# The sum over the experts turned by VectorE's 32x32 transpose and a scratch in DRAM, in place of four TensorE transposes

## The chip, the cores and the metric

The kernel runs on one core of one Trainium2 chip. The metric is the device time of one execution in microseconds; lower is better. TensorE's clock has two levels here, 1.2 and 2.4 GHz; the profile gives the granted clock as a share of the higher one.

## The reference

The input is 16 sequences of 512 tokens with 128 features. Each sequence goes through two layers, each wrapped in layer norms:

```
x = x + layernorm(attn(layernorm(x)))     # attn: project to 64 states, a complex scan over time, project back, + D * u
x = x + layernorm(ffn(layernorm(x)))      # ffn: 8 experts, all of them computed for every token

g = x @ w_gate[e];  u = x @ w_up[e]       # 128 -> 512 for each expert e
out = sum over e of cw[e] * ((silu(g) * u) @ w_down[e])       # 512 -> 128
cw  = softmax(x @ w_router) * softmax(x @ w_gating / 0.1), normalised over the experts
```

The change concerns only the last step: the layer norm of `out`, its addition to the residual and the store.

## The kernel before, in words

A chunk is one sequence of 512 tokens; there are 16. Inside a chunk the experts run feature-major: features on the 128 partitions, 512 tokens along the free axis. A chunk has 32 **units** k = 0 to 31, four for each expert, each of 128 hidden features. In unit k TensorE makes `g` and `u` (three matmuls of 128x512 each, since every fp32 product is split into a high and a low part) and then the down projection `y` of unit k - 3 (three more). ScalarE makes `gate` = silu(g) and rounds `hid` to `hid_hi`; VectorE makes `hid` = gate * u, and `hid_lo` for half of the units; GpSimd makes `hid_lo` for the others (k mod 4 = 1 or 3). `g` and `u` each have two PSUM buffers, so u of unit k + 2 may not start before `hid` of unit k is done.

When the four units of an expert are through, VectorE's `weigh` multiplies `y` by the expert's token weights `cw_b` (into `acc` for expert 0, else into `y_part`) and GpSimd's `add_part` adds `y_part` to `acc`. The last addition of a chunk happens in unit 4 of the next chunk.

The rest runs between the units. What belongs to which unit is written out by hand in the tables `TENSOR_AT`, `SCALAR_AT`, `VECTOR_AT` and `GPSIMD_AT` (lines 44 to 52). In chunk c they hold, first, the attention layer and the routing of chunk c + 1 ("the mix"), and second, the end of chunk c - 1 ("the fin steps"), which are what the change touches:

- TensorE, unit 10, `turn_out`: four 128x128 transposes of `acc` to the PSUM tile `n_ps`, so that tokens lie on the partitions.
- VectorE, unit 10, `fin_stats` (four BN_STATS on `n_ps`) and `fin_mean_var` (five small operations); unit 11, `fin_shifts`, after GpSimd's `fin_rsqrt`.
- ScalarE, units 14 and 15, `fin_scale`: four activations from `n_ps` to `o_sb`.
- GpSimd, unit 14, `fin_residual`: adds `x1`.
- SyncE, after the fifth `spread_cw` of the chunk, `store_out`.

`n_ps` is one PSUM tile that the mix uses for its own turns as well. SyncE issues all transfers in the order of its code: in a chunk the load of the next input, the store of the weights `cw_t` to a scratch, and eight `spread_cw`, each of which broadcasts one row of weights over all partitions, and waits until its buffer (one of four) is free.

Ahead of the first chunk there is a start (about 45 us) in which VectorE builds the table `trig` and runs the mix of chunk 0. TensorE has little to do there and is kept busy with matmuls whose results nobody reads: `keep_warm(n)` with the counts in `WARM`, and one call of `keep_warm_mixed`.

Of the kernel before, what the change touches and what calls it, by code (L numbers as in the profile page):

```python
# [47 lines left out]
VECTOR_AT = {"weights": 1, "stats_x": 1, "var_x": 2, "norm_x": 3, "lo_x": 7, "enter": 8, "scan": 9,  # L48
             "fin_stats": 10, "fin_var": 10, "fin_shift": 11, "leave": 12, "lo_w": 13, "y": 15, "stats_y": 16, "var_y": 16,
             "shift": 18, "stats_x1": 22, "var_x1": 22, "norm_x1": 24, "lo_xe": 26, "softmax": 27, "exps": 30,  # L50
             "products": 31}
GPSIMD_AT = {"rstd_x": 2, "fin_rstd": 11, "fin_add": 14, "rstd_y": 16, "residual": 18, "rstd_x1": 22}
LN_EPS = 1e-5
# [4 lines left out]
SMALL = 32  # L58
PROJ = P + D + 2 * E

POOL_LO = (1, 3)
# [15 lines left out]
def build(nc, x_in, proj_in, a_in, sines_in, d_in, wgate_in, wup_in, wdown_in, out):  # L77
# [5 lines left out]
    wdown_v = wdown_in.rearrange("e (b p) h -> e p b h", p=P)  # L83

    cw_dram = nc.dram_tensor("cw_scratch", [2, E * NT, P], f32, kind="Internal").ap()

    with ExitStack() as ctx:
# [28 lines left out]
        z_sb = sb("z_sb", [P, NT, D])  # L116
        x1 = sb("x1", [P, 2, NT, D])
        o_sb = sb("o_sb", [P, NT, D])
        trig = sb("trig", [P, SEQ])

# [25 lines left out]
        w_hi_done, w_lo_done = sem("w_hi_done"), sem("w_lo_done")  # L146
        const_ready, flat_ready = sem("const_ready"), sem("flat_ready")
        proj_split, omega_ready, trig_link, trig_ready = sem("proj_split"), sem("omega_ready"), sem("trig_link"), sem("trig_ready")
# [31 lines left out]
        def _(sp):  # L180
# [16 lines left out]
            def spread_cw(c, par, e, first):  # L197
# [39 lines left out]
        def _(pe):  # L237
# [28 lines left out]

            def keep_warm_mixed():


                y, w, x = y_ps[1], proj_hi[:, 0:P], act_hi[:]  # L270
                flat = hid_hi[:, 0, :]
                for i in range(4):
                    nc.tensor.matmul(y[0:32, :], w[:, 0:32], x, start=True, stop=True)
                for i in range(4):
                    nc.tensor.matmul(y[:], proj_hi[0:NS, 0:P], act_hi[0:NS, :], start=True, stop=True)
                for i in range(4):
                    nc.tensor.matmul(y[:], w, act_hi[:, 0:1].broadcast_to([P, SEQ]), start=True, stop=True)
                for off in (0, 4, 8):
                    for i in range(4):
                        nc.tensor.matmul(y[:, 0:SEQ - 8], w, act_hi[:, off:off + SEQ - 8], start=True, stop=True)  # L280
                pe.wait_ge(flat_ready, 2)
                for i in range(4):
                    nc.tensor.matmul(y[:], flat[:, 0:P], flat, start=True, stop=True)
                keep_warm(3)

# [19 lines left out]
            def mix_turn_y(c, first):  # L305
                pe.wait_ge(y_ready, c + 1)
                if not first:
                    pe.wait_ge(fin_z, c - 1)
                turn(n_ps, lambda j: y_sb[:, j * P:(j + 1) * P]).then_inc(y_turned, 1)
# [17 lines left out]

            def turn_out(c, par, tail=False, last=False):
                pe.wait_ge(part_added, ADDS * (c + 1))
                if last:  # L330
                    pe.wait_ge(fin_z, c)
                elif tail:
                    pe.wait_ge(cw_t_ready, c + 2)
                else:
                    pe.wait_ge(act_lo_ready, 2 * c + 5)
                turn(n_ps, lambda j: acc[:, par, j * P:(j + 1) * P]).then_inc(fin_turned, 1)
# [48 lines left out]
            def body(c, par, first, last):  # L385
                for k in range(UNITS):
# [9 lines left out]
                    if not last:  # L396
# [18 lines left out]
            turn_out(NCHUNK - 1, (NCHUNK - 1) % 2, last=True)  # L415


        @block.scalar
        def _(act):
# [131 lines left out]
        def _(dve):  # L551
# [86 lines left out]
            def mix_stats_x1(c, par):  # L638
                dve.wait_ge(x1_ready, c + 1)
                measure(lambda j: x1[:, par, j, :], stats, mix_link)  # L640

            def mix_norm_x1(c, par):
                dve.wait_ge(rstd_ready, 3 * c + 3)
                normalise(xn, lambda j: x1[:, par, j, :]).then_inc(xn_ready, 1)

# [45 lines left out]
            def mix_weights(c):  # L691
# [9 lines left out]
                                        wide(den[:], E), ALU.mult).then_inc(cw_ready, 1)  # L701

            def fin_stats(c):
                dve.wait_ge(fin_turned, c + 1)
                measure(lambda j: n_ps[:, j * P:(j + 1) * P], stats2, fin_link)
# [161 lines left out]
            def body(c, par, first, last):  # L867
                for k in range(UNITS):
# [16 lines left out]
                    if not last:  # L885
# [36 lines left out]
                        if k == VECTOR_AT["products"]:  # L922
                            mix_products(c + 1)
                    if not first:
                        if k == VECTOR_AT["fin_stats"]:
                            fin_stats(c - 1)
                        if k == VECTOR_AT["fin_var"]:
                            fin_mean_var(c - 1)
                        if k == VECTOR_AT["fin_shift"]:
                            fin_shifts(c - 1)  # L930
# [10 lines left out]
                                    ALU.add).then_inc(part_added, 1)  # L941
            fin_stats(NCHUNK - 1)
            fin_mean_var(NCHUNK - 1)
            fin_shifts(NCHUNK - 1)
            for j in range(NT):
                if j < NT - 1:
                    dve.wait_ge(fin_tile, j + 1)
                else:
                    dve.wait_ge(fin_z, NCHUNK)
                last = nc.vector.tensor_tensor(o_sb[:, j, :], x1[:, end, j, :], o_sb[:, j, :], ALU.add)  # L950
            last.then_inc(fin_ready, 1)
# [3 lines left out]
        def _(pool):  # L955
# [10 lines left out]
            def mix_residual(c, par):  # L966
                pool.wait_ge(z_ready, c + 1)
                nc.gpsimd.tensor_tensor(x1[:, par], x_sb[:], z_sb[:], ALU.add).then_inc(x1_ready, 1)

# [4 lines left out]
            def fin_residual(c, par):  # L974
                pool.wait_ge(fin_z, c + 1)
                nc.gpsimd.tensor_tensor(o_sb[:], x1[:, par], o_sb[:], ALU.add).then_inc(fin_ready, 1)

# [101 lines left out]
```

## Time and profile before

| | before |
|---|---|
| three runs, us | 1173.66, 1175.09, 1175.84 |
| median, us | 1175.09 |
| the profiled execution's own time, us | 1174.75 |
| span of its trace, us | 1172.9 |
| mean granted clock of TensorE | 0.992 |
| TensorE matmul busy, share of the span | 97% |
| VectorE busy | 79% |
| ScalarE busy | 58% |
| GpSimd busy | 54% |
| DMA queue of SyncE, share of 16 engines | 13.4% |

The profiled execution took 0.34 us less than the median, and 1.85 us of its time lie outside its span. Matmuls overlap in the records (a 128x512 matmul is shown with some 390 ns, while the next one starts 227 ns after it), so the cost of a matmul is read from the distance of starts or from the chain that ended last, not from its own duration.

### The profile page before, as it was taken

To read this page: it belongs to the slowest core of one execution; us is meant where nothing else is said; L and a number is where in the kernel's file an instruction comes from. 1 tells how busy PE (TensorE), PEld (TensorE's weight loads), DVE (VectorE), ACT (ScalarE), POOL (GpSimd) and SP (SyncE) were. 2 spreads that over 40 slices of the span, in tenths; PEclk is the share of its full clock that TensorE was granted. 3 is DMA by queue.
4 is the path that set the end of the run, shared out by engine and by line. 5 is a ranking of instruction groups with operands and counts; after the bars stand their busy time and mean duration, and the time that the engine had idled before them with its cause. 6 is when DMAs were issued, how large, how long until landed. Compare 5 with 4: busy or idle time off the path is not lost.

```text
span 1172.9 us, 16867 instructions
## 1 busy us (share of the span) xinstructions
PE 1143.5 (97%) x5190; PEld 943.3 (80%) x5190; DVE 928.8 (79%) x2032; ACT 677.4 (58%) x1293; POOL 636.2 (54%) x496
## 2 busy tenths in 40 slices
PE   5899999999999999999999999999999999999996
PEld 4678888888888888888888888888888888888885
DVE  8788787787878878787887878778787887878665
ACT  3366565656556566565656656565655656556553
POOL 4467464555546455564655546455554645556453
PEclk8999999999999999999999999999999999999999
DMA  4230110101111020110101111010111102011110
GB/s 122 64 111 25 46 45 34 40 20 46 46 43 49 1 72 19 45 46 37 41 15 57 35 46 46 32 42 19 46 46 41 50 1 72 19 46 37 37 46 10
DMA packets 43097, 49.75 MB, mean 42 GB/s; under 512 B 3424, under 2 KB 24576, under 8 KB 43008
## 3 DMA queue, kind: packets, MB, share of 16 engines
q1 hardware_dynamic: 43008, 48.67, 13.4%
q8 instruction: 43, 0.70, 0.2%
q14 instruction: 46, 0.38, 0.1%
HBM read 44.20 MB, written 4.46 MB: 41 GB/s over the span
## 4 chain that ended last, share of the span: by engine, by line
PE 95%; DVE 3%; issue 1%; POOL 0%; ACT 0%; DMA 0%; POOLq 0%; SPq 0%; ACTq 0%; DVEq 0%
PE g L240 10%; PE u L240 10%; PE u L242 10%; PE u L241 10%; PE g L242 10%; PE g L241 10%; PE y L242 10%; PE y L240 10%; PE y L241 10%; PE n_ps L247 2%; PE m_ps L240 1%; PE m_ps L242 1%; PE m_ps L241 1%; PE y L263 1%; PE m_ps L321 1%
## 5 line engine op out<-in xcount | busy, mean ns | idle before, releaser
L982 POOL TENSOR_TENSOR hid_lo<-hid,hid_hi 128x512 fp32r<-128x512 f32 x255 | 342.2, 1342 | 394.5 <-ACT hid_hi L483 394.3
L477 ACT ACTIVATE gate<-g 128x512 f32<-128x512 f32 x512 | 306.3, 598 | 363.0 <-PE g L242 360.5
L723 DVE TENSOR_TENSOR hid<-gate,u 128x512 f32<-128x512 f32 x512 | 349.2, 682 | 176.9 <-ACT gate L477 121.6
L483 ACT ACTIVATE hid_hi<-hid 128x512 fp32r<-128x512 f32 x512 | 320.6, 626 | 29.4 <-DVE hid L723 28.7
L240 PE MATMUL g<-xe_hi,w_hi 128*128 128x512 f32 x512 | 207.8, 406 | 0.0
L729 DVE TENSOR_TENSOR hid_lo<-hid,hid_hi 128x512 fp32r<-128x512 f32 x257 | 205.7, 800 | 0.4
L240 PE MATMUL u<-xe_hi,w_hi 128*128 128x512 f32 x512 | 200.0, 391 | 2.3 <-DVE hid L723 2.3
L240 PE MATMUL y<-hid_hi,w_hi 128*128 128x512 f32 x512 | 199.8, 390 | 0.2 <-ACT hid_hi L483 0.2
L242 PE MATMUL y<-hid_hi,w_lo 128*128 128x512 f32 x512 | 199.8, 390 | 0.0
L242 PE MATMUL g<-xe_hi,w_lo 128*128 128x512 f32 x512 | 199.6, 390 | 0.0
L241 PE MATMUL g<-xe_lo,w_hi 128*128 128x512 f32 x512 | 199.6, 390 | 0.0
L242 PE MATMUL u<-xe_hi,w_lo 128*128 128x512 f32 x512 | 199.5, 390 | 0.0
L241 PE MATMUL y<-hid_lo,w_hi 128*128 128x512 f32 x512 | 199.3, 389 | 0.0
L241 PE MATMUL u<-xe_lo,w_hi 128*128 128x512 f32 x512 | 199.2, 389 | 0.0
L989 POOL TENSOR_TENSOR acc<-acc,y_part 128x512 f32<-128x512 f32 x111 | 159.2, 1434 | 3.1 <-DVE y_part L738 3.1
L240 PEld LDWEIGHTS u<-xe_hi,w_hi 128*128 128x128 f32 x512 | 96.1, 188 | 23.5 <-DVE hid L723 3.1
L240 PEld LDWEIGHTS y<-hid_hi,w_hi 128*128 128x128 f32 x512 | 96.1, 188 | 20.8 <-ACT hid_hi L483 0.6
L242 PEld LDWEIGHTS g<-xe_hi,w_lo 128*128 128x128 f32 x512 | 96.2, 188 | 20.6
L242 PEld LDWEIGHTS u<-xe_hi,w_lo 128*128 128x128 f32 x512 | 96.1, 188 | 20.5
L242 PEld LDWEIGHTS y<-hid_hi,w_lo 128*128 128x128 f32 x512 | 96.1, 188 | 20.5
L241 PEld LDWEIGHTS u<-xe_lo,w_hi 128*128 128x128 f32 x512 | 96.1, 188 | 20.3
L241 PEld LDWEIGHTS y<-hid_lo,w_hi 128*128 128x128 f32 x512 | 96.1, 188 | 20.1
(155 smaller groups left out, 1146.6 us busy)
## 6 DMA issues: line engine op xcount, KB each, us to landing
cw_b<-cw_scratch SPq DMA_DIRECT2D x128, 256.0 KB, 3.6
x_sb<-x_in SPq DMA_DIRECT2D x16, 256.0 KB, 4.0
x_out<-o_sb SPq DMA_DIRECT2D x16, 256.0 KB, 2.3
stage<-wgate_in SPq DMA_DIRECT2D x8, 256.0 KB, 2.7
stage<-wup_in SPq DMA_DIRECT2D x8, 256.0 KB, 3.0
stage<-wdown_in SPq DMA_DIRECT2D x8, 256.0 KB, 3.6
cw_scratch<-cw_t SPq DMA_DIRECT2D x16, 16.0 KB, 1.4
proj<-proj_in SPq DMA_DIRECT2D x1, 136.0 KB, 2.5
```

What stands on the lines that cost most here:

```text
L240: nc.tensor.matmul(dst, w_h, x_h, start=start, stop=False)
L241: nc.tensor.matmul(dst, w_h, x_l, start=False, stop=False)
L242: return nc.tensor.matmul(dst, w_l, x_h, start=False, stop=stop)
L247: last = nc.tensor.transpose(dst[:, j * P:(j + 1) * P], src(j), ident[:])
L263: last = nc.tensor.matmul(y_ps[1][:, 0:2 * P].rearrange("p (a b) -> p a b", a=2), ident[:], ident[:].unsqueeze(1).broadcast_to([P, 2, P]), ...
L321: last = nc.tensor.matmul(m_ps[:, at:at + 2 * E], xe_lo[:, par, t], router[:, 0, :], start=False, stop=True)
L477: nc.scalar.activation(gate[:, k % 2, :], g_ps[k % 2][:], ACT.Silu).then_inc(gate_ready, 1)
L483: nc.scalar.activation(hid_hi[:, k % RING, :], hid[:, k % RING, :], ACT.Copy).then_inc(hi_ready, 1)
L723: nc.vector.tensor_tensor(hid[:, k % RING, :], gate[:, k % 2, :], u_ps[k % 2][:], ALU.mult).then_inc(hid_ready, 1)
L729: nc.vector.tensor_tensor(hid_lo[:, k % RING, :], hid[:, k % RING, :], hid_hi[:, k % RING, :].bitcast(f32), ALU.subtract).then_inc(lo_dve, 1)
L982: nc.gpsimd.tensor_tensor(hid_lo[:, k % RING, :], hid[:, k % RING, :], hid_hi[:, k % RING, :].bitcast(f32), ALU.subtract).then_inc(lo_pool, 1)
L989: nc.gpsimd.tensor_tensor(acc[:, par, :], acc[:, par, :], y_part[:, e % 2, :], ALU.add).then_inc(part_added, 1)
```

## The change

For chunks 0 to 14 the four TensorE transposes are replaced. In unit 6 of the next chunk VectorE transposes `acc` in 32x32 blocks into `acc_t` (`fin_turn`). Each block is now turned in itself but stands in the wrong place. SyncE then stores `acc_t` with four transfers (`turn_blocks`), each from 32 partitions, in pieces of 32 fp32 values (128 bytes), to a scratch in DRAM in token-major order, and loads the scratch back as `ffn`, tokens on partitions (`load_blocks`). The fin steps read `ffn` in SBUF instead of `n_ps`, and are moved: `fin_stats` and `fin_mean_var` from unit 10 to 14, `fin_shifts` from 11 to 15, `fin_rsqrt` from 11 to 15, `fin_scale` from 14 and 15 to 19 and 20, `fin_residual` from 14 to 21, and `store_out` to the end of the chunk's eight `spread_cw`. `x1` gets three buffers instead of two. The last chunk keeps its TensorE transposes. In the start, `keep_warm_mixed` is replaced by `keep_warm(18)`, and 24 matmuls (`keep_warm_split`) are put where TensorE was idle before the first projection; the two VectorE instructions that filled an operand of `keep_warm_mixed` are gone.

```diff
-TENSOR_AT = {"turn_cw": 4, "turn_x": 5, "bu": 9, "turn_out": 10, "c": 15, "turn_y": 16, "turn_xe": 26,
+TENSOR_AT = {"turn_cw": 4, "turn_x": 5, "bu": 9, "c": 15, "turn_y": 16, "turn_xe": 26,
-SCALAR_AT = {"cw_t": 3, "hi_x": 8, "du": 8, "hi_w": 13, "fin_a": 14, "fin_b": 15, "z_a": 18, "z_b": 18,
+SCALAR_AT = {"cw_t": 3, "hi_x": 8, "du": 8, "hi_w": 13, "fin_a": 19, "fin_b": 20, "z_a": 18, "z_b": 18,
...
+FIN_STORED = 16 * (D // SMALL)
+X1S = 3
...
+    out_dram = nc.dram_tensor("out_scratch", [SEQ, D], f32, kind="Internal").ap()
...
+            def turn_blocks(c):
+                sp.wait_ge(fin_turned, c + 1)
+                if c > 0:
+                    sp.wait_ge(fin_loaded, 16 * c)
+                blocks = out_dram.rearrange("(b c) (a r) -> a c b r", c=SMALL, r=SMALL)
+                for a in range(D // SMALL):
+                    sp.dma_start(blocks[a], acc_t[a * SMALL:(a + 1) * SMALL, :].rearrange("c (b r) -> c b r", r=SMALL)
+                                 ).then_inc(fin_stored, 16)
+
+            def load_blocks(c):
+                sp.wait_ge(fin_stored, FIN_STORED * (c + 1))
+                if c > 0:
+                    sp.wait_ge(fin_z, c)
+                sp.dma_start(ffn[:], out_dram.rearrange("(j p) d -> p j d", p=P)).then_inc(fin_loaded, 16)
...
                 for e in range(E):
                     spread_cw(c, par, e, first)
-                    if e == 4 and not first:
+                    if e == 3 and not first:
+                        turn_blocks(c - 1)
+                        load_blocks(c - 1)
+                    if e == E - 1 and not first:
                         store_out(c - 1)
...
-            def keep_warm_mixed():
...
+            def keep_warm_split():
+                w = proj_hi[:, 0:P]
+                for i in range(8):
+                    nc.tensor.matmul(y_ps[1][:, 0:SEQ - P], w, act_hi[:, 0:SEQ - P], start=True, stop=True)
+                for i in range(8):
+                    nc.tensor.matmul(y_ps[1][:].rearrange("p (a t) -> p a t", a=2), w,
+                                     act_hi[:, 0:HALF].unsqueeze(1).broadcast_to([P, 2, HALF]), start=True, stop=True)
+                for i in range(8):
+                    nc.tensor.matmul(y_ps[1][:].rearrange("p (t a) -> p t a", a=2), w,
+                                     act_hi[:, 0:HALF].unsqueeze(2).broadcast_to([P, HALF, 2]), start=True, stop=True)
...
             keep_warm(WARM[1])
+            pe.wait_ge(act_hi_ready, 1)
+            keep_warm_split()
             pe.wait_ge(proj_split, 2)
...
-            keep_warm_mixed()
+            keep_warm(WARM[3])
...
-                    if k == TENSOR_AT["turn_out"] and not first:
-                        turn_out(c - 1, 1 - par, tail=last)
...
-                    last = nc.scalar.activation(o_sb[:, j, :], n_ps[:, j * P:(j + 1) * P], ACT.Identity,
+                    last = nc.scalar.activation(o_sb[:, j, :], ffn[:, j, :], ACT.Identity,
...
+            def fin_turn(c, par):
+                dve.wait_ge(part_added, ADDS * (c + 1))
+                if c > 0:
+                    dve.wait_ge(fin_stored, FIN_STORED * c)
+                nc.vector.transpose(acc_t[:], acc[:, par, :]).then_inc(fin_turned, 1)
+
             def fin_stats(c):
+                dve.wait_ge(fin_loaded, 16 * (c + 1))
+                measure(lambda j: ffn[:, j, :], stats2, fin_link)
```

TensorE, around unit 10 of a chunk that has a chunk before it (y of unit 7, then what follows up to g of unit 11). Before:

```order
L240 MATMUL y<-hid_hi,w_hi 128x512
L241 MATMUL y<-hid_lo,w_hi 128x512
L242 MATMUL y<-hid_hi,w_lo 128x512
L247 MATMUL n_ps<-ident,acc 128x128 x4
L240 MATMUL g<-xe_hi,w_hi 128x512
L241 MATMUL g<-xe_lo,w_hi 128x512
L242 MATMUL g<-xe_hi,w_lo 128x512
```

and now:

```order
L263 MATMUL y<-hid_hi,w_hi 128x512
L264 MATMUL y<-hid_lo,w_hi 128x512
L265 MATMUL y<-hid_hi,w_lo 128x512
L263 MATMUL g<-xe_hi,w_hi 128x512
L264 MATMUL g<-xe_lo,w_hi 128x512
L265 MATMUL g<-xe_hi,w_lo 128x512
```

The four transposes are gone; the matmuls on both sides are the same. VectorE, from the last step of the scan in unit 12 (`v_sb`) over the `hid` of unit 13 to that of unit 16, before:

```order
L619 TENSOR_TENSOR v_sb<-sum_sb,trig 128x512
L723 TENSOR_TENSOR hid<-gate,u 128x512
L729 TENSOR_TENSOR hid_lo<-hid,hid_hi 128x512
L624 TENSOR_TENSOR act_lo<-v_sb,act_hi 128x512
L723 TENSOR_TENSOR hid<-gate,u 128x512 x2
L729 TENSOR_TENSOR hid_lo<-hid,hid_hi 128x512
L628 TENSOR_TENSOR y_sb<-m_ps,y_sb 128x512
L723 TENSOR_TENSOR hid<-gate,u 128x512
```

and now, from the `hid` of unit 14:

```order
L743 TENSOR_TENSOR hid<-gate,u 128x512
L566 BN_STATS stats<-ffn 128x6 x4
L573 TENSOR_TENSOR mv<-stats 128x8
L574 TENSOR_TENSOR var_eps<-stats 128x4
L578 TENSOR_TENSOR mv<-mv,pair_mean 128x8
L579 SCALAR_TENSOR_TENSOR var_eps<-var_eps 128x4
L584 SCALAR_TENSOR_TENSOR var_eps<-mv,var_eps 128x4
L743 TENSOR_TENSOR hid<-gate,u 128x512
L749 TENSOR_TENSOR hid_lo<-hid,hid_hi 128x512
L638 TENSOR_TENSOR y_sb<-m_ps,y_sb 128x512
L600 SCALAR_TENSOR_TENSOR shift<-mv,rstd 128x4
L743 TENSOR_TENSOR hid<-gate,u 128x512
```

The four BN_STATS and the five small operations of the fin steps now stand between the `hid` of units 14 and 15, and `fin_shifts` (the one on `shift`) behind `y_sb`; before they stood in units 10 and 11. SyncE, one whole chunk, before:

```order
L182 DMA x_sb<-x_in 128x4x128
L195 DMA cw_scratch<-cw_t 32x128
L204 DMA cw_b<-cw_scratch 128x512 x5
L208 DMA x_out<-o_sb 128x4x128
L204 DMA cw_b<-cw_scratch 128x512 x3
```

and now:

```order
L187 DMA x_sb<-x_in 128x4x128
L200 DMA cw_scratch<-cw_t 32x128
L209 DMA cw_b<-cw_scratch 128x512 x4
L217 DMA out_scratch<-acc_t 32x16x32 x4
L224 DMA ffn<-out_scratch 128x4x128
L209 DMA cw_b<-cw_scratch 128x512 x4
L228 DMA x_out<-o_sb 128x4x128
```

The four stores and the load stand between the fourth and the fifth broadcast, and the store of the output moved behind the eighth.

## Rows read from the trace of the kernel before

**Rows 1.** The page: span, and busy us (share of the span) by engine

```profile
span 1172.9 us, 16867 instructions
PE 1143.5 (97%) x5190; PEld 943.3 (80%) x5190; DVE 928.8 (79%) x2032; ACT 677.4 (58%) x1293; POOL 636.2 (54%) x496
```

**Rows 2.** Busy time in a window: start:end, length, then busy us by engine

```profile
120.00:1100.00 980.00, 980.00 (x4488) 812.05 (x4487) 789.09 (x1719) 582.84 (x1112) 533.82 (x408) 1.00 0.12 38
```

**Rows 3.** The chain that ended last, in order of time: start us, us, what

```profile
212.65 0.44 PE n_ps L247 x4
226.02 0.44 PE n_ps L247 x4
...
295.69 0.44 PE n_ps L247 x4
```

**Rows 4.** Timeline, units 4 to 7 of a chunk: start us, us, instruction [idle before]

```profile
201.84 1.81 POOL L989 TENSOR_TENSOR acc<-acc,y_part 128x512 f32<-128x512 f32 x1
...
203.19 0.69 DVE L723 TENSOR_TENSOR hid<-gate,u 128x512 f32<-128x512 f32 x1 [0.70 <-ACT gate L477]
205.24 0.69 DVE L723 TENSOR_TENSOR hid<-gate,u 128x512 f32<-128x512 f32 x1 [1.36 <-PE u L242]
```

**Rows 5.** Groups by line: VectorE operations of 128x512 from SBUF to SBUF

```profile
L615 DVE TENSOR_TENSOR_SCAN sum_sb<-v_sb 128x512 f32<-128x512 f32 x16 | 20.6, 1288 | 0.0
...
L624 DVE TENSOR_TENSOR act_lo<-v_sb,act_hi 128x512 fp32r<-128x512 f32 x15 | 11.3, 752 | 0.0
...
L759 DVE CAST hid_hi<-hid 128x512 fp32r<-128x512 f32 x1 | 0.4, 428 | 0.0
```

**Rows 6.** DMA: queue, issues, and the last store's window (last columns: clock, DMA share, GB/s)

```profile
q1 hardware_dynamic: 43008, 48.67, 13.4%
...
x_sb<-x_in SPq DMA_DIRECT2D x16, 256.0 KB, 4.0
x_out<-o_sb SPq DMA_DIRECT2D x16, 256.0 KB, 2.3
...
1170.30:1172.90 2.60, 0.50 0.34 101
```

**Rows 7.** Timeline of VectorE, fin_stats at unit 10, then units 14 to 16

```profile
214.15 0.89 DVE L556 BATCH_NORM_STATS2 stats<-n_ps 128x6 f32<-128x128 f32 x4
...
215.73 0.69 DVE L723 TENSOR_TENSOR hid<-gate,u 128x512 f32<-128x512 f32 x1
...
222.71 0.69 DVE L723 TENSOR_TENSOR hid<-gate,u 128x512 f32<-128x512 f32 x1 [0.80 <-ACT gate L477]
...
224.02 0.69 DVE L628 TENSOR_TENSOR y_sb<-m_ps,y_sb 128x512 f32<-128x512 f32 x1
225.43 0.69 DVE L723 TENSOR_TENSOR hid<-gate,u 128x512 f32<-128x512 f32 x1 [0.72 <-PE u L242]
```

**Rows 8.** Timeline, ScalarE and VectorE and TensorE, unit 15 and units 18 to 21

```profile
222.99 0.80 ACT L468 ACTIVATE o_sb<-n_ps,shift,rstd 128x128 f32<-128x128 f32 x2
...
231.81 1.50 ACT L441 ACTIVATE z_sb<-n_ps,shift,rstd 128x128 f32<-128x128 f32 x4 [1.42 <-DVE shift L590]
...
234.20 0.62 ACT L477 ACTIVATE gate<-g 128x512 f32<-128x512 f32 x1
...
233.84 0.69 DVE L723 TENSOR_TENSOR hid<-gate,u 128x512 f32<-128x512 f32 x1 [2.06 <-ACT gate L477]
...
233.16 0.39 PE L240 MATMUL u<-xe_hi,w_hi 128*128 128x512 f32 x1
...
235.20 0.39 PE L240 MATMUL u<-xe_hi,w_hi 128*128 128x512 f32 x1
```

**Rows 9.** The start: windows of 1 us, and VectorE's last step before mix_c

```profile
17.00:18.00 1.00, 0.00 (x0) 0.00 (x0) 1.00 (x2) 0.00 (x0) 1.00 (x2) 0.89 0.00 0
...
42.00:43.00 1.00, 1.00 (x4) 0.86 (x5) 0.38 (x2) 0.06 (x1) 0.00 (x0) 0.50 0.31 16
...
27.57 0.42 DVE L838 TENSOR_TENSOR act_lo<-v_sb,act_hi 128x256 fp32r<-128x256 f32 x1
```

More of the change, by code:

```diff
@@ L41 @@
 PIECES = WCOLS // F
-TENSOR_AT = {"turn_cw": 4, "turn_x": 5, "bu": 9, "turn_out": 10, "c": 15, "turn_y": 16, "turn_xe": 26,
+TENSOR_AT = {"turn_cw": 4, "turn_x": 5, "bu": 9, "c": 15, "turn_y": 16, "turn_xe": 26,
              "logits": 27}
-SCALAR_AT = {"cw_t": 3, "hi_x": 8, "du": 8, "hi_w": 13, "fin_a": 14, "fin_b": 15, "z_a": 18, "z_b": 18,
+SCALAR_AT = {"cw_t": 3, "hi_x": 8, "du": 8, "hi_w": 13, "fin_a": 19, "fin_b": 20, "z_a": 18, "z_b": 18,
              "hi_xe": 26, "silus": 28}
 VECTOR_AT = {"weights": 1, "stats_x": 1, "var_x": 2, "norm_x": 3, "lo_x": 7, "enter": 8, "scan": 9,
-             "fin_stats": 10, "fin_var": 10, "fin_shift": 11, "leave": 12, "lo_w": 13, "y": 15, "stats_y": 16, "var_y": 16,
+             "fin_turn": 6, "fin_stats": 14, "fin_var": 14, "fin_shift": 15, "leave": 12, "lo_w": 13, "y": 15, "stats_y": 16, "var_y": 16,
              "shift": 18, "stats_x1": 22, "var_x1": 22, "norm_x1": 24, "lo_xe": 26, "softmax": 27, "exps": 30,
              "products": 31}
-GPSIMD_AT = {"rstd_x": 2, "fin_rstd": 11, "fin_add": 14, "rstd_y": 16, "residual": 18, "rstd_x1": 22}
+GPSIMD_AT = {"rstd_x": 2, "fin_rstd": 15, "fin_add": 21, "rstd_y": 16, "residual": 18, "rstd_x1": 22}
 LN_EPS = 1e-5
@@ L116, in build @@
         z_sb = sb("z_sb", [P, NT, D])
-        x1 = sb("x1", [P, 2, NT, D])
+        x1 = sb("x1", [P, X1S, NT, D])
         o_sb = sb("o_sb", [P, NT, D])
+        acc_t, ffn = sb("acc_t", [P, SEQ]), sb("ffn", [P, NT, D])
         trig = sb("trig", [P, SEQ])
@@ L265, in keep_warm @@
                 return last
-            def keep_warm_mixed():
[L270 to L284, printed above, removed]
+            def keep_warm_split():
[8 more added lines that the diff above has]
+                                     act_hi[:, 0:HALF].unsqueeze(2).broadcast_to([P, HALF, 2]), start=True, stop=True)
             def mix_turn_x(c):
@@ L306, in mix_turn_y @@
                 pe.wait_ge(y_ready, c + 1)
-                if not first:
-                    pe.wait_ge(fin_z, c - 1)
                 turn(n_ps, lambda j: y_sb[:, j * P:(j + 1) * P]).then_inc(y_turned, 1)
@@ L326, in mix_turn_cw, with turn_out_last @@
                 nc.tensor.transpose(n_ps[:, 0:P], cw_pad[:], ident[:]).then_inc(cw_turned, 1)
-            def turn_out(c, par, tail=False, last=False):
+            def turn_out_last(c, par):
                 pe.wait_ge(part_added, ADDS * (c + 1))
[L330 to L335, printed above, removed]
+                pe.wait_ge(cw_t_ready, c + 1)
                 turn(n_ps, lambda j: acc[:, par, j * P:(j + 1) * P]).then_inc(fin_turned, 1)
@@ L414, in _ @@
                 down(NCHUNK - 1, k, False, last_unit=k == UNITS - 1)
-            turn_out(NCHUNK - 1, (NCHUNK - 1) % 2, last=True)
+            turn_out_last(NCHUNK - 1, (NCHUNK - 1) % 2)
         @block.scalar
@@ L639, in mix_stats_x1 @@
                 dve.wait_ge(x1_ready, c + 1)
[L640 removed]
+                measure(lambda j: x1[:, c % X1S, j, :], stats, mix_link)
             def mix_norm_x1(c, par):
                 dve.wait_ge(rstd_ready, 3 * c + 3)
[L644 removed]
+                normalise(xn, lambda j: x1[:, c % X1S, j, :]).then_inc(xn_ready, 1)
             def mix_lo_xe(c, par):
@@ L924, in body @@
                     if not first:
+                        if k == VECTOR_AT["fin_turn"]:
+                            fin_turn(c - 1, 1 - par)
                         if k == VECTOR_AT["fin_stats"]:
@@ L941, in _ @@
                                     ALU.add).then_inc(part_added, 1)
-            fin_stats(NCHUNK - 1)
+            fin_stats_last(NCHUNK - 1)
             fin_mean_var(NCHUNK - 1)
@@ L949, in _ @@
                     dve.wait_ge(fin_z, NCHUNK)
-                last = nc.vector.tensor_tensor(o_sb[:, j, :], x1[:, end, j, :], o_sb[:, j, :], ALU.add)
+                last = nc.vector.tensor_tensor(o_sb[:, j, :], x1[:, (NCHUNK - 1) % X1S, j, :], o_sb[:, j, :], ALU.add)
             last.then_inc(fin_ready, 1)
@@ L967, in mix_residual @@
                 pool.wait_ge(z_ready, c + 1)
-                nc.gpsimd.tensor_tensor(x1[:, par], x_sb[:], z_sb[:], ALU.add).then_inc(x1_ready, 1)
+                nc.gpsimd.tensor_tensor(x1[:, c % X1S], x_sb[:], z_sb[:], ALU.add).then_inc(x1_ready, 1)
             def fin_rsqrt(c):
@@ L975, in fin_residual @@
                 pool.wait_ge(fin_z, c + 1)
-                nc.gpsimd.tensor_tensor(o_sb[:], x1[:, par], o_sb[:], ALU.add).then_inc(fin_ready, 1)
+                nc.gpsimd.tensor_tensor(o_sb[:], x1[:, c % X1S], o_sb[:], ALU.add).then_inc(fin_ready, 1)
             def hid_low(c, k, first):
```

7 lines of the change are left out of this document (3 added, 4 removed).

## The prediction

> **What bounds the kernel now.** I read the page first. TensorE's matmuls fill 97% of a span of 1172.9 us, VectorE 79% of it [rows 1]. Next the busy time of the long middle stretch: from 120 to 1100 us TensorE is busy for 980.00 of 980.00 us at full granted clock [rows 2], so outside the start and the tail there is no idle time of TensorE to win, and a chunk gets shorter only if TensorE is given less to do. The chain that ended last agrees: it goes from matmul to matmul, and the turn of `y_sb` in it comes back after 295.69 - 226.02 = 69.67 us, the length of a chunk [rows 3]. The other engines matter only where they are late enough to stop TensorE, so the timelines of VectorE and ScalarE around each moved step are read for one thing, how much time is left before the matmul that needs them.
>
> **What is removed.** Four transposes of `acc` take 0.44 us of the chain [rows 3]. They go from 15 of 16 chunks, since the last keeps its own: 15 x 0.44 = 6.6 us. They are shown in the chain with nothing beside them, and TensorE has no gap before the next g, so all of it comes off if nothing else becomes late.
>
> **The block transpose on VectorE (unit 6).** No such operation is in the trace. The nearest, 128x512 from SBUF to SBUF, run from 0.43 us (the cast, the fastest) through 0.75 us (a tensor_tensor) to 1.29 us (the scan) [rows 5]. I take 0.7. It stands between the `hid` of units 6 and 7, where VectorE is idle for 1.36 us waiting for TensorE's u; the last addition to `acc`, for which it has to wait, ends at 201.84 + 1.81 = 203.65, and the `hid` before it is over at about 203.8 [rows 4]. So it starts at once, and even 1.29 us fits into the gap. It costs the path nothing. Without the gap it would cost nothing either until the `hid` behind it is about two units late. What ends is at about 204.5 on the clock of that chunk.
>
> **The transfers.** Four stores, 32 partitions x 16 pieces = 512 pieces of 128 bytes each, 2048 in all, then a load of 512 pieces of 512 bytes like that of `x_sb`. The path needs `ffn` in unit 14, behind a `hid` after which VectorE is free at 222.71 - 0.80 = 221.9 now [rows 7], and 0.44 earlier once the transposes are gone, or a little before that: about 221.2. The final store of the output has 512 pieces of 512 bytes too; it lands in 2.3 us, with 0.34 x 2.60 = 0.88 us of work for each of the 16 engines: 27 ns for each of its 32 pieces [rows 6]. The mean over all packets of the kernel is 0.134 x 1172.9 / (43008 / 16) = 58 ns [rows 6], for packets of 1.1 KB. The stores are 128 pieces per engine, so 3.5 us at 27 ns and 7.4 us at 58 ns; I take 7.4, as the pieces are small. With the fixed part of a store, 2.3 - 0.9 = 1.4 us, and 4.0 us for the load [rows 6], `ffn` is there at 204.5 + 1.4 + 7.4 + 4.0 = 217.3, or 213.4 at the low price, 4 to 8 us before it is wanted. SyncE stands still for all of this, and what is queued behind it are the fifth broadcast of weights, whose row is first used in unit 24, some 20 us on, and the later ones; nobody waits for these. Behind the eighth, `store_out` waits for GpSimd's addition in unit 21; behind that stands the load of the next input, used one unit into the next chunk, again about ten units off.
>
> The Trainium skill, "DMA: Bandwidth & Descriptors", section Specifications, says that transfers under 512 bytes fall below line rate because the engine reads, modifies and writes; "VectorE: DVE Perf Modes", section The three transpose paths, warns that a plain copy that transposes by strides is 19 times slower than the crossbar's. No row here shows either. Taken on the 27 ns piece as an estimate, 19 times would be 0.5 us a piece and 66 us of stores in a chunk, which would make the change a disaster; but the pieces here are 32 contiguous values, the elements having been turned by VectorE before, so I do not take it.
>
> **The moved fin steps.** In unit 10, statistics and variance take 214.15 to 215.73, 1.58 us, on a VectorE that is then late for the next `hid` [rows 7]. That goes. In unit 14 they come between two `hid` with 0.80 us of idle time, ahead of `y_sb`, before which and after which VectorE waits again, 0.72 us [rows 7]. TensorE needs `y_sb` for its turn at 226.02, now 0.44 earlier at 225.6, and it is ready at 224.02 + 0.69 = 224.7 [rows 3, 7]. Started at 221.2, `fin_mean_var` is over at 222.8, and the `hid` of unit 15, which could start at 222.71 - 0.44 = 222.3, starts half a microsecond late; the idle time ahead of `y_sb` and behind it takes this up. Nothing on the path. On ScalarE the four activations, 0.80 us a pair, move from units 14 and 15 to 19 and 20, right behind the mix's own four of 1.50 us, after which ScalarE is catching up [rows 8]. The `hid` of unit 19 ends at 234.53 and TensorE wants it at 235.20: 0.7 us to spare, the tightest place. The first pair comes after the silu of that unit, so it delays the next: silu of unit 20 from 234.20 to 235.0, its `hid` to about 236.3; u of unit 22 starts at 235.20 + (235.20 - 233.16) = 237.24 [rows 8]: 0.9 us to spare. `hid_lo` of unit 19 on GpSimd keeps about as much. Cost 0; without this cover it would be up to 0.8 us per pair.
>
> **The start.** TensorE is idle in the window at 17 us, and its clock falls to half there [rows 9]. The 24 new matmuls fill about 24 x 0.227 = 5 us ahead of that, at the distance of matmuls in a unit, (235.20 - 233.16) / 9 = 0.227 us [rows 8]. The chain there runs through VectorE, though: its last step before the second projection ends at 27.57 + 0.42 = 27.99 [rows 9], whatever TensorE's clock. If the clock stays up, 0.2 us are won in the projection; if it falls later instead, its three matmuls cost 3 x 0.227 = 0.7 us more at the lower level. In the window at 42 us, just ahead of the first unit, the clock is at half again [rows 9]; six passes of keep_warm and a first g at that level are worth some 1.5 us either way. I take 0, with -1.5 to +1.5.
>
> **The sum.** 1174.75 (the profiled execution: span 1172.9 and 1.85 around it) - 6.6 = 1168.15. The median is 0.34 above that execution, so against the median 1168.5. I give 1168.4.
>
> **The rivals.** *Slow small pieces (slower).* If `ffn` is late, VectorE, which works in order, stands at `fin_stats` with `hid` of unit 15, `hid_lo` and `y_sb` queued behind it, 1.58 + 3 x 0.6 = 3.4 us of work that must end by 225.6. So `ffn` may come up to 222.2. This leaves 222.2 - 4.0 - 1.4 - 204.5 = 12.3 us for 128 pieces: 96 ns each is where it turns. A write that first reads costs two mean packets, 116 ns: 20 ns too much, 2.6 us a chunk, 15 chunks, +38 - 6.6, so 1207. For it: no row has small writes at all. Against: even a mean packet is well below. The read-modify-write of the skill would be this case. Chance 0.10.
>
> *The wait moves to units 19 to 22 (about no gain).* For it: 0.7 to 0.9 us to spare, and operations of VectorE that are held up while GpSimd works; GpSimd's addition has moved there too. If it stops TensorE by 0.3 to 0.5 us a chunk, 4.5 to 7.5 us come back: 1173 to 1176. Against: nowhere in the middle stretch is TensorE stopped now, with the same 0.7 us. Chance 0.12; a third of this with most of the gain kept.
>
> *The start gives it back:* priced above, within 1.5 us; it is inside the likeliest case's range, not a case of its own.
>
> **How the numbers follow.** The plain case, everything hidden, has the remaining 0.78. Its own range is 1168.4 with -1.5 and +1.5 for the start and about 0.5 for the runs: 1166.4 to 1170.4. To leave out no more than 2 in 10 the range reaches up into the second case, to 1171.8. A measurement of this kernel tells 0.2%, 2.35 us, from no change. Faster by more than that (below 1172.7): all of the plain case and a third of the second, 0.82. Within it: half of the second, 0.06. Slower: the first rival and the rest, 0.12.
>
> **What would show it.** In the profile after: chunks of 69.67 - 0.44 = 69.2 us; the middle stretch again without idle time of TensorE; the transpose on VectorE at 0.4 to 1.3 us with an idle gap left behind it; the stores landed within 9 us and `fin_stats` not waiting for the load; the second projection in the start at 28 us. Wrong would be: a wait of `fin_stats` for the transfer of `ffn` of more than about 1 us, or waits of TensorE for `hid` or `hid_lo` in units 19 to 22, or the first g later than 45 us by more than 1.5.

## The result, and the profile after

| | before | after |
|---|---|---|
| median of 9 runs each, taken together, us | 1174.46 | 1170.8 |
| lowest and highest | 1173.18, 1176.11 | 1169.59, 1171.37 |
| ratio | | 0.9967 [0.9957, 0.9977] |
| the profiled execution, its own time and its span | 1174.75, 1172.9 | 1171.27, 1169.4 |

The changed kernel is faster by 3.66 us, where 6.6 were forecast. The interval of the ratio allows 2.7 to 5.1 us. The time is inside the range given, 2.4 us above the forecast, but 0.4 us above the range of the prediction's plain case, which ended at 1170.4. Its page, with the columns of [rows 1, 6]:

```profile
span 1169.4 us, 16900 instructions
PE 1144.2 (98%) x5156; PEld 940.8 (80%) x5156; DVE 946.0 (81%) x2045; ACT 673.4 (58%) x1293; POOL 640.3 (55%) x496
...
q1 hardware_dynamic: 82608, 56.54, 16.4%
...
x_out<-o_sb SPq DMA_DIRECT2D x16, 256.0 KB, 2.2
out_scratch<-acc_t SPq DMA_DIRECT2D x60, 64.0 KB, 2.3
ffn<-out_scratch SPq DMA_DIRECT2D x15, 256.0 KB, 2.7
```

And the middle stretch, as in [rows 2]:

```profile
120.00:1100.00 980.00, 980.00 (x4451) 807.82 (x4450) 809.49 (x1738) 580.75 (x1115) 538.97 (x409) 1.00 0.16 46
```

TensorE has fewer instructions, VectorE is busy for 17 us more, the packets have almost doubled, and still TensorE is the engine that is never without work in the middle. Busy time, though, does not show whether each matmul took as long as before; the chain does. First the turn of `y_sb` of chunk 0 in the kernel before, then in the changed kernel, and there one chunk from turn to turn (the turn of `y_sb`, the one for `xe`, that of the next input, and `y_sb` again):

```profile
85.89 0.44 PE n_ps L247 x4
...
87.19 0.44 PE n_ps L270 x4
...
226.50 0.44 PE n_ps L270 x4
247.40 0.51 PE n_ps L270 x4
271.53 0.44 PE n_ps L270 x4
295.88 0.44 PE n_ps L270 x4
```

This shows two things against the forecast. A chunk lasts 295.88 - 226.50 = 69.38 us, not 69.2: of [rows 3]'s 69.67 only 0.29 is gone. And the turn of chunk 0 stands at 87.19, where the chain of before has it at 85.89: the start lost 1.30 us. From there to the end 4.8 us were won. 4.8 - 1.3 = 3.5 is the difference of the two spans.

The steps on which the prediction spent most words, on the timeline of VectorE and SyncE of the changed kernel:

```profile
204.75 0.70 DVE L717 STREAM_TRANSPOSE acc_t<-acc 128x512 f32<-128x512 f32 x1
205.48 2.74 SPq L217 DMA_DIRECT2D out_scratch<-acc_t  x4
206.19 0.69 DVE L743 TENSOR_TENSOR hid<-gate,u 128x512 f32<-128x512 f32 x1 [0.73 <-ACT gate L487]
...
210.47 0.38 SPq L224 DMA_DIRECT2D ffn<-out_scratch  x1
...
222.19 0.86 DVE L566 BATCH_NORM_STATS2 stats<-ffn 128x6 f32<-128x128 f32 x4
```

The block transpose takes 0.70 us and leaves 0.73 us of its gap idle. The load is issued 210.47 - 204.75 = 5.7 us after the transpose began, and lands 2.7 us later, at 213.2; `fin_stats` comes 9 us after that and waits for nothing. The transfers are not where the missing 2.9 us are.

### The profile page after: what moved, and what is told of

The parts are those of the page before. It is cut to its first block, busy times and chain, and to the rows that moved or that the text cites. A ratio compares the mean times of both kernels' runs of the same rounds, so it can differ in the third digit from the quotient of the medians.

```text
span 1169.4 us, 16900 instructions
## 1 busy us (share of the span) xinstructions
PE 1144.2 (98%) x5156; PEld 940.8 (80%) x5156; DVE 946.0 (81%) x2045; ACT 673.4 (58%) x1293; POOL 640.3 (55%) x496
## 4 chain that ended last, share of the span: by engine, by line
PE 95%; DVE 3%; issue 1%; POOL 0%; ACT 0%; DMA 0%; POOLq 0%; SPq 0%; ACTq 0%; DVEq 0%
PE g L263 10%; PE u L263 10%; PE u L265 10%; PE u L264 10%; PE g L264 10%; PE g L265 10%; PE y L263 10%; PE y L265 10%; PE y L264 10%; PE n_ps L270 2%; PE m_ps L263 1%; PE m_ps L265 1%; PE m_ps L264 1%; PE m_ps L335 1%; PE y L286 1%; PE m_ps L336 1%
## 5 line engine op out<-in xcount | busy, mean ns | idle before, releaser
L749 DVE TENSOR_TENSOR hid_lo<-hid,hid_hi 128x512 fp32r<-128x512 f32 x257 | 202.3, 787 | 1.8
```

The lines of the kernel that those rows point to most:

```text
L749: nc.vector.tensor_tensor(hid_lo[:, k % RING, :], hid[:, k % RING, :], hid_hi[:, k % RING, :].bitcast(f32), ALU.subtract).then_inc(lo_dve, 1)
```

## The experiments

All were timed beside the kernel before on their own chip; its medians there were 1174.86 (the first four kernels below the changed one), 1176.01 (the next four) and 1174.88 (the last four). "Turn 0" is the turn of `y_sb` of chunk 0 in the chain, which reads the start; "chunk" is the mean distance of that turn over the middle chunks; "rest" is what the profiled execution's span has left behind turn 0, which leaves the start out.

| kernel | median (lowest to highest, n), us | ratio to before | turn 0 | chunk | rest |
|---|---|---|---|---|---|
| before | 1174.46 (1173.18 to 1176.11, 9) | 1 | 85.89 | 69.67 | 1087.01 |
| after | 1170.8 (1169.59 to 1171.37, 9) | 0.9967 [0.9957, 0.9977] | 87.19 | 69.37 | 1082.21 |
| after, old start | 1168.37 (1167.83 to 1169.89, 5) | 0.9952 [0.9939, 0.9964] | 84.42 | 69.35 | 1082.08 |
| before, new start | 1175.65 (1175.07 to 1176.2, 11) | 1.001 [1.0001, 1.0019] | 86.68 | | 1087.12 |
| scale and addition later | 1168.08 (1167.9 to 1168.99, 5) | 0.9948 [0.9935, 0.996] | 85.99 | 69.21 | 1080.11 |
| addition later | 1168.51 (1167.92 to 1168.96, 5) | 0.9949 [0.9936, 0.9961] | 87.09 | 69.20 | 1080.01 |
| addition later, old start | 1167.8 (1166.14 to 1168.09, 5) | 0.9933 [0.9921, 0.9946] | 85.91 | 69.21 | 1080.09 |
| stores four times | 1170.32 (1169.69 to 1171.14, 4) | 0.9957 [0.9942, 0.9973] | 86.25 | 69.38 | 1082.45 |
| stores eight times | 1287.82 (1285.74 to 1289.51, 4) | 1.0956 [1.0939, 1.0973] | 86.17 | | |
| filler up to the turn | 1169.16 (1168.98 to 1169.38, 5) | 0.9947 [0.9935, 0.996] | 84.90 | 69.37 | 1082.30 |
| without the split matmuls | 1170.09 (1169.47 to 1171.06, 5) | 0.9957 [0.9944, 0.9969] | 87.05 | 69.35 | 1082.15 |
| addition later, filler to the turn | 1167.13 (1166.98 to 1168.43, 5) | 0.9932 [0.9919, 0.9946] | 84.91 | 69.23 | 1080.59 |
| the same without the split matmuls | 1166.62 (1166.43 to 1166.78, 5) | 0.9926 [0.9913, 0.9938] | 84.82 | 69.21 | 1079.98 |
| before, new start, filler to the turn | 1173.87 (1173.13 to 1174.43, 11) | 0.9991 [0.9983, 1.0] | 84.95 | | 1087.15 |

### The start, alone and taken out

The changed kernel with the old start, and the old kernel with the new one:

```diff
-            keep_warm_split()
...
-            keep_warm(WARM[3])
+            keep_warm_mixed()
...
+            nc.vector.memset(hid[:, 0, :], 0.5).then_inc(flat_ready, 1)
+            nc.vector.tensor_copy(hid_hi[:, 0, :], hid[:, 0, :]).then_inc(flat_ready, 1)
```

> The changed kernel with the start of before put back: keep_warm_mixed and its two VectorE instructions instead of the 24 new matmuls and keep_warm(18); the chunks are those of the changed kernel. In the profiles so far the start ends 1.30 us later in the changed kernel, because TensorE's clock comes back to full at 48.0 us instead of 46.0, while the chunks give 4.8 us. Theory A, the new start is the cause: the first turn of y_sb is back at about 85.9 us and the median about 1.3 us below the changed kernel, 1169.5. Theory B, the moment at which the clock comes back scatters from execution to execution whatever the start: median within 0.6 us of the changed kernel, 1170.8, and spans that scatter by up to 2 us in both.

> The kernel before with only the new start; the chunks and the four TensorE transposes are those of before. Theory A: about 1.3 us above the kernel before, 1175.8. Theory B: within 0.6 us of it, 1174.5.

The new start costs about 1.2 us on the old kernel (1.001, with an interval from 0.1 to 2.2 us), and taking it out of the changed one gives 1.8 us by the ratios (0.9967 to 0.9952, whose intervals overlap). In both chains the turn at about 30 us stands level (30.02 before, 30.06 after); the windows behind it show where the time goes, first of the changed kernel:

```profile
30.00:41.00 11.00, 8.72 (x41) 7.29 (x41) 7.25 (x26) 2.28 (x6) 6.95 (x7) 1.00 0.25 73
38.00:40.00 2.00, 0.49 (x3) 0.09 (x1) 0.84 (x3) 0.00 (x0) 1.67 (x2) 1.00 0.31 94
...
42.00:48.00 6.00, 6.00 (x17) 4.73 (x17) 1.07 (x3) 1.19 (x2) 0.00 (x0) 0.50 0.57 175
```

then of the one with the old start:

```profile
30.00:41.00 11.00, 11.00 (x36) 7.66 (x34) 7.82 (x25) 1.74 (x5) 6.96 (x7) 0.69 0.24 73
...
42.00:48.00 6.00, 5.84 (x30) 4.76 (x31) 2.66 (x7) 2.27 (x5) 0.00 (x0) 1.00 0.58 175
```

and of the kernel before, which has the old start too:

```profile
42.00:48.00 6.00, 6.00 (x26) 5.02 (x27) 2.16 (x6) 1.20 (x2) 0.00 (x0) 0.74 0.57 175
```

`keep_warm(18)` is over at 38.5 us, TensorE is nearly idle until the turn for `xe` at 41.9, and then the first matmuls of the experts run with a granted clock of 0.50, the lower level of 1.2 GHz, until 48: 17 of them in a stretch that holds 30 at 2.4 GHz. In the run with the old start the filler ran at a mixed clock, took longer, and reached up to 41.3; the window from 42 to 48 us has 1.00. But the old start is not safe either: the profiled execution of before had 0.74 there, and so did that of the kernel with the addition later and the old start, both with turn 0 at 85.9. So the old start can come out as in the second profile or as in the third. That the start differs from one execution to the next was the rival, and both hold. Over the profiles the clock of 42 to 48 us and turn 0 go together: 0.50 and 0.51 with 87.19 and 87.05, 0.72 to 0.74 with 85.89 to 86.68, 1.00 with 84.42.

### The split matmuls left out

```diff
-            pe.wait_ge(act_hi_ready, 1)
-            keep_warm_split()
```

> The changed kernel without the 24 new matmuls of the start (keep_warm_split); keep_warm(18) stays. Theory: what counts in the start is how long TensorE is busy ahead of the first unit, from 30 to 41 us, so these 24 matmuls between 13 and 18 us are worth little: median within 0.7 us of the changed kernel, 1170.8. Rival: with TensorE idle from 13 to 22 us the clock comes back late and slow filler reaches 41 us by itself, as in one run of the old start: 1169.3 or less.

The same time, and turn 0 at 87.05 for 87.19. The matmuls fill the gap ahead of the first projection, but the chain there runs through VectorE, as the prediction said.

### Filler up to the turn

```diff
-WARM = (13, 3, 6, 18, 3)
+WARM = (13, 3, 6, 24, 3)
```

> The changed kernel with keep_warm(24) instead of keep_warm(18) behind the first turn of y_sb, so that TensorE is busy until about 41.2 us instead of 38.5, and idles hardly at all before the first unit. Theory: the granted clock then stays full from 40 to 48 us, three passes of keep_warm and the first g and u run at the upper level, and the first turn of y_sb in unit 16 comes at 84.4 to 85.0 us (87.2 in the changed kernel, 84.4 in the run with the old start, where a low clock from 30 to 34 us had stretched the same kind of filler to 41.3). Time 1168.3 to 1169.0. Rival: the clock falls anyway (it is another idle stretch that counts), or the longer filler holds up the turn: 1170.8 or more.

```profile
30.00:41.00 11.00, 10.95 (x53) 9.57 (x53) 7.26 (x25) 2.28 (x6) 6.96 (x7) 1.00 0.25 73
...
42.00:48.00 6.00, 5.84 (x30) 4.62 (x31) 2.72 (x8) 1.74 (x4) 0.00 (x0) 1.00 0.60 175
```

Six more matmuls nobody reads, no gap, a clock of 1.00 and turn 0 at 84.90. In the runs the ratio goes from 0.9967 to 0.9947. In all four kernels with this filler the clock of 42 to 48 us is 1.00 and turn 0 stands between 84.82 and 84.95. The median is slightly above the 1169.0 that was expected at most. So the gap ahead of the turn was the cause of the loss in the start: with it the clock of 42 to 48 us lay between 0.50 and 0.74 in nine profiles, without it at 1.00 in five. It makes some of the scatter too: these five runs lie within 0.4 us and those of the best version below within 0.35, where the nine of the changed kernel spread over 1.8; but two others with the filler still spread over 1.3 and 1.45.

### The fin steps, both later, and the addition alone

For the 0.29 instead of 0.44 us a chunk the suspects were the steps moved into units 19 to 21: ScalarE's two pairs, or GpSimd's addition.

```diff
-SCALAR_AT = {..., "fin_a": 19, "fin_b": 20, ...}
+SCALAR_AT = {..., "fin_a": 23, "fin_b": 24, ...}
-GPSIMD_AT = {..., "fin_add": 21, ...}
+GPSIMD_AT = {..., "fin_add": 26, ...}
```

> The changed kernel with fin_scale in units 23 and 24 instead of 19 and 20, and fin_residual in unit 26 instead of 21. Theory: of the 0.44 us that the removed transposes give in each chunk, 0.15 come back in units 26 and 27, because the fin steps in units 19 to 21 make VectorE's normalisation of x1 in unit 24 late (245.0 us instead of 243.0 on the clock of the chunk), so that the turn for xe and the logits wait. If so, the chunk takes 69.22 us instead of 69.37, and the time is 15 x 0.15 = 2.2 us below the changed kernel, 1168.6. Rival: the lateness comes from fin_stats in unit 14, or from the missing 0.44 us itself; then the chunk stays at 69.37 and the time at 1170.8.

And with the second of the two lines alone:

> As the run before, but only GpSimd's fin_residual is moved (unit 26 instead of 21); fin_scale stays on ScalarE in units 19 and 20. If GpSimd's addition is the cause (it delays hid_lo of unit 21 and the reciprocal root of x1's variance), nearly all of the 0.15 us a chunk comes back: 1168.8. If ScalarE's two pairs are the cause (they delay the silu and so hid of units 20 to 22), it stays near 69.37 us a chunk, 1170.8. I expect half: the normalisation starts some 1 us earlier, and the chunk takes about 69.28.

I had given each half of the loss, and that missed: the addition alone brings the chunk to 69.20, and moving ScalarE's pairs as well adds nothing that can be measured. The same four turns of the chain with the addition in unit 26:

```profile
226.33 0.44 PE n_ps L270 x4
247.23 0.44 PE n_ps L270 x4
271.23 0.44 PE n_ps L270 x4
295.53 0.44 PE n_ps L270 x4
```

From the turn of `y_sb` to that for `xe` both kernels take 20.90 us. From there to the turn of the next input it is 24.00 here and 24.13 in the changed kernel, of which 0.07 is the longer turn itself (0.51 for 0.44); the next piece is 24.30 here and 24.35 there. What makes the difference stands on the timelines of GpSimd and VectorE; of the changed kernel, units 21 to 25:

```profile
239.12 1.75 POOL L995 TENSOR_TENSOR o_sb<-x,o_sb 128x512 f32<-128x512 f32 x1
240.82 1.29 POOL L1001 TENSOR_TENSOR hid_lo<-hid,hid_hi 128x512 fp32r<-128x512 f32 x1
...
242.76 1.02 POOL L983 TENSOR_TENSOR rstd<-var_eps,half 128x4 f32<-128x4 f32 x1 [0.65 <-DVE var_eps L584]
...
241.12 1.01 DVE L573 TENSOR_TENSOR mv<-stats 128x8 f32<-128x8 f32 x1
...
245.03 2.17 DVE L595 TENSOR_SCALAR xn<-x,mv,rstd 128x128 f32<-128x128 f32 x4
```

and of the one with the addition in unit 26:

```profile
239.24 1.48 POOL L1001 TENSOR_TENSOR hid_lo<-hid,hid_hi 128x512 fp32r<-128x512 f32 x1 [0.22 <-ACT hid_hi L493]
241.78 1.02 POOL L983 TENSOR_TENSOR rstd<-var_eps,half 128x4 f32<-128x4 f32 x1 [1.05 <-DVE var_eps L584]
...
248.81 1.29 POOL L995 TENSOR_TENSOR o_sb<-x,o_sb 128x512 f32<-128x512 f32 x1
...
240.99 0.17 DVE L573 TENSOR_TENSOR mv<-stats 128x8 f32<-128x8 f32 x1
...
244.06 2.17 DVE L595 TENSOR_SCALAR xn<-x,mv,rstd 128x128 f32<-128x128 f32 x4
```

In unit 21 the addition stands ahead of GpSimd's `hid_lo` and pushes it from 239.24 to 240.82 (the two chunks stand 0.17 us apart). VectorE's small step of the variance of `x1` now falls beside that `hid_lo` and takes 1.01 us for 0.17, in each of the chunks 1 to 14 (with the addition in unit 26 it is 0.17 in all of them). It ends at 242.13, when that `hid_lo` does (242.11). On the clock of the chunk the root on GpSimd behind it is 0.8 us later, and the normalisation `xn` too; it ends at 245.03 + 2.17 = 247.20, just as TensorE comes to the turn at 247.40. With the addition in unit 26 it ends at 246.23, for a turn at 247.23: a microsecond early. The list of waits counts what TensorE's weight loads lost, in the changed kernel:

```profile
PEld n_ps L270 <- DVE xn L595: 7.1, 16, 1.9
...
PEld m_ps L335 <- issue: 3.4, 15, 0.2
```

and with the addition in unit 26:

```profile
PEld n_ps L270 <- DVE xn L595: 3.0, 2, 1.9
...
PEld m_ps L335 <- issue: 0.2, 1, 0.2
```

The first entry is the transposes waiting for `xn`, the second the logits' loads of 0.2 us each. The two waits that are left stand in chunk 0, which has no fin steps; the other 14 are the chunks 1 to 14, which have both the fin steps and the mix.

Both remedies were put together, first with the old start, then with the longer filler, and the filler also on the kernel before, whose transposes stay on TensorE.

> The two causes together: GpSimd's fin_residual in unit 26, and the start of before. If they are independent, the time is that of the run with only the addition moved, 1168.5, less the 1.1 to 1.8 us that the old start was worth: 1166.7 to 1167.4. Against the kernel before this is the whole 15 x 0.44 = 6.6 us and a little more.

> The changed kernel with both mends: GpSimd's fin_residual in unit 26, and keep_warm(24). Theory, the two are independent: 1169.16 - 2.2 = 1166.9, with the first turn of y_sb at 84.9 us and chunks of 69.21 us.

> The kernel before, its four TensorE transposes in every chunk, with the new start and keep_warm(24). It is the fair rival of the run before in this list: the same start, only the turn differs. Theory: the first turn of y_sb at 84.4 to 84.9 us instead of 85.9, so 1173.5; and the difference to the run with both mends is 15 x 0.45 = 6.7 us, all of what the removed transposes take.

The first came out slightly above what was expected. The last two differ only in the replaced transposes and where the fin steps stand, with a start of the same length in both (84.91 and 84.95): 1173.87 - 1167.13 = 6.74 us, that is 0.45 for each of 15 chunks, with about 1.9 us either way by the intervals of the two ratios. This is the term of the prediction, measured by itself. By the rest behind turn 0 it is 1087.15 - 1080.59 = 6.6; but that profiled execution has 0.4 us more behind its last chunk than the other four with the addition in unit 26, whose rest is 1080.0 to 1080.1; against those it is 7.0 to 7.2.

### Repeated stores

The prediction's rival of slow small pieces turned at 96 ns a piece. The stores were issued four and eight times, each time to a scratch of its own, and the load waits for all:

```diff
-                for a in range(D // SMALL):
-                    sp.dma_start(blocks[a], ...
+                for n, a in [(n, a) for n in range(REPEAT) for a in range(D // SMALL)]:
+                    sp.dma_start(blocks[n, a], ...
```

> The changed kernel with the four stores of the turned blocks issued four times, to four different scratches, and the load from the last: 16 stores a chunk, the load waits for all. From the trace of the changed kernel: four stores from 205.5 to about 210.4, of which 2.3 are the landing of one, so some 0.7 us each; 16 of them take until about 218.8, the load until 221.5. Theory (ffn may come up to about 222.2): no change of the chunk, 69.4 us, and of the time, 1170.8 within 0.6. Rival (the path has less room than I reckoned, or the small pieces disturb the broadcasts): more than 1 us slower.

> As the run before with the stores issued eight times: 32 stores until about 230, ffn at about 232.6 on the clock of the chunk, 10 us after the point from which fin_stats holds VectorE. Theory: the wait appears at fin_stats and is passed on to TensorE, some 9 to 10 us in each of 15 chunks, so 1305 to 1320. Rival: no more than a few us, if VectorE's order has more room than I think.

SyncE and VectorE with four times the stores:

```profile
204.56 9.35 SPq L218 DMA_DIRECT2D out_scratch<-acc_t  x16
...
215.33 0.38 SPq L225 DMA_DIRECT2D ffn<-out_scratch  x1
...
221.34 0.86 DVE L567 BATCH_NORM_STATS2 stats<-ffn 128x6 f32<-128x128 f32 x4
```

and with eight times, SyncE, VectorE, a window among the stores and two behind them, and the waits:

```profile
213.84 18.25 SPq L218 DMA_DIRECT2D out_scratch<-acc_t  x32
233.51 0.39 SPq L225 DMA_DIRECT2D ffn<-out_scratch  x1
...
236.33 0.87 DVE L567 BATCH_NORM_STATS2 stats<-ffn 128x6 f32<-128x128 f32 x4 [5.68 <-DMA ffn<-out_scratch]
...
216.00:230.00 14.00, 14.00 (x64) 11.58 (x63) 11.31 (x17) 9.53 (x17) 6.38 (x5) 1.00 0.69 118
...
240.00:241.00 1.00, 1.00 (x5) 0.95 (x5) 1.00 (x2) 0.00 (x0) 0.59 (x1) 0.52 0.00 0
241.00:242.00 1.00, 1.00 (x4) 0.76 (x3) 1.00 (x4) 0.00 (x0) 0.11 (x1) 0.50 0.00 0
...
DVE stats L567 <- DMA ffn<-out_scratch: 93.8, 15, 8.3
...
PE n_ps L271 <- DVE y_sb L639: 76.4, 15, 6.5
```

Sixteen stores are hidden: `ffn` is asked for at 215.33, there by about 218.1, and `fin_stats` begins at 221.34 without a wait. Thirty-two are not: VectorE stands for 93.8 us in all, and TensorE for the `y_sb` behind it, 76.4 us. The 117 us more than the changed kernel are 7.8 a chunk, below the 9 to 10 that I had expected. They are not all wait: in this chunk TensorE stood still for 5.0 us until 239.84, and then its granted clock was 0.50 to 0.52 up to 243. Over the whole span it was busy for 1180.4 us where the changed kernel has 1144.2, so 36 of the 117 us went into slower matmuls (mean granted clock 0.959 for 0.992), and about 81 us into idle time. A store takes 18.25 / 32 = 0.57 us here, with the 16 DMA engines 0.69 busy: 0.39 us of each engine's time for its 32 pieces, 12 ns a piece, and at most 0.57 / 32 = 18 ns if the engines and not the issuing set the pace, which these runs do not tell apart.

### The best version

The longer filler, the addition in unit 26 and no split matmuls:

> GpSimd's fin_residual in unit 26, keep_warm(24), and no keep_warm_split. Theory: chunks of 69.21 us and a full clock before the first unit, as with keep_warm_split: 1169.2 - 15 x 0.15 = 1166.9. Rival: without the split the clock is low when keep_warm(24) begins, the filler is too long and holds up the turn: 1168 or more.

It takes 1166.62 us, 0.9926 [0.9913, 0.9938] of before, 4.2 us below the changed kernel's median, and 4.8 by the two ratios, since the kernel before was timed anew on this chip.

## Why the prediction was right, and where it was off

**The bound, and what was removed.** Right. TensorE has no idle time in the middle in either kernel, and with all else equal the 15 sets of transposes are worth 6.74 us by the medians and 7.0 by the rest behind turn 0 (forecast: 6.6).

**The block transpose.** 0.706 us in the mean of 15, taken as 0.7. Hidden, as forecast; the gap it left is 0.73 us.

**The transfers.** The mechanism held, the price taken was too high: `ffn` landed at 213.2, the low end (213.4), not at 217.3. The load took 2.7 us for the 4.0 taken. That a piece of 128 bytes would cost as much as a mean packet of the kernel was the mis-sized term: in the sum's own form the four stores give (210.47 - 205.45 - 1.4) / 128 = 28 ns for the 58 taken, the low price, and the repeated stores 12 to 18. The changed kernel's stores land in 2.3 us, the same as the output's in [rows 6], with pieces of a quarter of their length. The Trainium skill's rule that transfers under 512 bytes fall below line rate ("DMA: Bandwidth & Descriptors", Specifications) agrees with the rows by direction: 12 ns for 128 bytes against 27 ns for 512 [rows 6] is 1.8 times the engine time for each byte. Whether reading before writing is the reason no run shows, and here it cost nothing. The factor 19 ("VectorE: DVE Perf Modes", The three transpose paths) was rightly left aside, but untested: no run stores single elements by strides. The rival of slow pieces needs more than four times the stores: at sixteen nothing waits, at thirty-two it is true.

**The moved fin steps.** Here a step failed. ScalarE's pairs, called the tightest place, cost nothing: moved away they gave nothing. The rival that the wait moves to units 19 to 22 was right in kind and wrong in place: it is the case "with most of the gain kept", to which the prediction gave a third of 0.12. Of the signs that it named as wrong none appears (in the middle TensorE waits neither for `hid` nor for `hid_lo`); only the chunk of 69.2 us that it asked for fails. I had set GpSimd's addition against `hid` and `hid_lo` of its own unit, and not against the other chain that passes through GpSimd: statistics of `x1`, root, `xn`, the turn for `xe`, the logits. With the addition in unit 21 that chain lost its reserve, and TensorE pays in units 26 and 27: 69.37 - 69.20 = 0.17 us in each of the 14 chunks that have the fin steps and the mix, 2.2 us by the rest behind turn 0 (1082.2 to 1080.0). The prediction had put this at 0.

**The start.** Taken as 0 with 1.5 either way; it cost 1.2 to 1.8 us by the ratios and 1.3 in the profiled execution. The clock at half ahead of the first unit was read from [rows 9] but given no sign. (The row at 17 us there shows 0.89 and not half; the clock was 0.50 in the windows behind it, from 18 to 22 us.) I should have looked at which filler ends when: `keep_warm(18)` ends over 3 us ahead of the turn for `xe`, and in the profiled starts with it alone the clock of 42 to 48 us was 0.50 to 0.72. That the split matmuls would win nothing was right.

**The sum.** Of the 6.6 us forecast, 3.66 came: 2.9 are missing. The column "rest" splits them with the start left out. It is 1087.01 to 1087.15 for the three kernels with all their TensorE transposes, 1082.08 to 1082.45 for the five with the addition in unit 21 whose transfers are hidden, and 1079.98 to 1080.11 for four of the five with it in unit 26. So the replacement was worth 7.0 us where 6.6 were forecast, the addition took back 2.2 where 0 was forecast, and the start 1.3 where 0 was forecast: 7.0 - 2.2 - 1.3 = 3.5, the difference of the two spans. That the time still fell inside the range owes something to its upper end, which was stretched to 1171.8 to take in part of the second rival: the two costs put at 0 add up to 3.5 us, and the gain was 0.4 us larger than forecast.

## What to carry to other kernels

When a step moves to another engine or unit, list every chain that passes through that engine behind it, not only the operation of the same unit, and compare each one's reserve with the step's length: a move of 1.3 us on an engine that is idle almost half the time cost a sixth of a microsecond of TensorE, in each chunk, five units later. Read from the windows where the filler that keeps TensorE's clock up ends: in these profiles the clock of the first real matmuls was full only where it reached to the turn ahead of them. And a transpose in blocks with the rest done by DMA was hidden here with each piece contiguous, since the elements were turned before they were stored, and with some 17 us from the block transpose to the first use, of which the way through DRAM needed 8.4. A copy that turns single elements was not tried.

## What the runs showed of the hardware

- A store of 512 pieces of 128 bytes took 0.57 us behind others like it, 115 GB/s, with the DMA engines 0.69 busy: 12 ns of engine time a piece, for 27 ns a piece of 512 bytes in the output's store. It lands in 2.3 us, like one of 512-byte pieces with four times the bytes.
- A VectorE operation on 128x8 elements took 1.01 us instead of 0.17 when it fell beside a GpSimd operation of 128x512. It happened at that place in each of the chunks 1 to 14 (mean of the 64 of its line: 0.61), and it ended when the GpSimd operation did.
- ScalarE's activation of 128x128 took 0.503 us when it read `ffn` from SBUF and 0.455 when it read `n_ps` from PSUM; VectorE's statistics 0.272 from SBUF and 0.284 from PSUM.
